# Dequantisation of the feed-forward weights: from the softmax attention's loop into the expert stage

## What is computed

```
x = x + tanh(g_xattn[0]) * linear_attention(layernorm(x), ctx)
x = x + tanh(g_ffn[0])   * experts(layernorm(x))              # 8 experts, top 2, plus a shared one
x = x + tanh(g_xattn[1]) * softmax_attention(layernorm(x), ctx)  # 16 heads, fake-quantised queries and output
x = x + tanh(g_ffn[1])   * feed_forward(layernorm(x), Wg, Wu, Wd)

def dequant_nvfp4(W_packed, scales, block=32):     # Wg, Wu, Wd come packed
    low  = W_packed & 15                           # two 4-bit codes per word
    high = W_packed >> 4 & 15
    idx  = stack([low, high])
    vals = LUT[idx]      # 0 .5 1 1.5 2 3 4 6, and the same negated for codes 8 to 15
    return vals * scales # one scale per 32 values
```

## Time and profile before

| | us |
|---|---|
| median of 3 runs (2783.67 to 2786.23) | 2785.93 |
| the profiled execution | 2784.78 |
| its span, first to last instruction | 2783.1 |
| PE busy | 2628.8 (94%) |
| DVE busy | 1835.6 (66%) |
| POOL busy | 1521.4 (55%) |
| ACT busy | 1487.8 (53%) |

### The profile page before, as it was taken

One profiled execution on the slowest core, in us unless ns is written; L12 is line 12 of the kernel. 1 busy time (PEld: TensorE's weight loads), 2 busy tenths in 40 slices (PEclk: granted clock), 3 DMA queues, 4 the chain that ended last, 5 costly groups with the idle time before them and its releaser, 6 DMA issues. The chain is left out here.

```text
span 2783.1 us, 63103 instructions
## 1 busy us (share of the span) xinstructions
PE 2628.8 (94%) x23470; PEld 2228.8 (80%) x23470; DVE 1835.6 (66%) x3075; ACT 1487.8 (53%) x2543; POOL 1521.4 (55%) x1547
## 2 busy tenths in 40 slices
PE   5999999999899997699999999999999999979998
PEld 3999999999765664488888888888888888858998
DVE  4888888888742225466667666666666666655654
ACT  2666666666321221366666666666666666643443
POOL 2988888888532111456656656656655655632322
PEclk9999999999989998799999999999999999989999
DMA  4554454454381112121121121111112112131000
GB/s 121 165 155 146 141 155 145 142 155 144 79 238 49 46 46 65 51 66 64 34 64 63 34 64 63 35 63 64 45 52 64 58 38 64 41 122 66 8 8 14
DMA packets 110936, 225.25 MB, mean 81 GB/s; under 512 B 32800, under 2 KB 81040, under 8 KB 106864
## 3 DMA queue, kind: packets, MB, share of 16 engines
q1 hardware_dynamic: 105536, 215.86, 25.8%
q0 software_dynamic: 3216, 8.29, 0.9%
q10 hardware_dynamic: 2112, 0.12, 0.1%
HBM read 193.24 MB, written 27.33 MB: 79 GB/s over the span
## 5 line engine op out<-in xcount | busy, mean ns | idle before, releaser
L1607 DVE TENSOR_SCALAR_CACHE_REDUCE a_prob<-a_s 112x1500 f32<-112x1500 f32 x256 | 440.1, 1719 | 116.4 <-PE a_s L1716 115.9
L1728 PEld LDWEIGHTS a_p<-ident,a_prob 112*125 112x125 f32 x3072 | 380.4, 188 | 112.1 <-issue 103.4
L1549 ACT COPY a_probT<-a_p 125x448 f32<-125x448 f32 x512 | 248.8, 534 | 375.3 <-PE a_p L1728 375.3
L1728 PE MATMUL a_p<-ident,a_prob 112*125 112x112 f32 x3072 | 445.6, 281 | 2.2 <-ACT a_prob L1542 1.4
L1542 ACT ACTIVATE a_prob<-a_prob,a_mxs 112x1500 f32<-112x1500 f32 x256 | 396.6, 1549 | 64.8 <-DVE a_prob L1607 64.8
L443 POOL TENSOR_TENSOR l_rows_lo<-l_raw,l_rows_hi 125x512 fp32r<-125x512 f32 x192 | 273.1, 1422 | 104.9 <-ACT l_rows_hi L478 104.9
L446 POOL TENSOR_TENSOR l_phik_lo<-l_phif,l_phik_hi 125x512 fp32r<-125x512 f32 x192 | 297.5, 1550 | 11.8 <-ACT l_phik_hi L484 11.8
L542 DVE TENSOR_TENSOR l_ctxT_lo<-l_rawT,l_ctxT_hi 128x500 fp32r<-128x500 f32 x192 | 214.5, 1118 | 94.9 <-ACT l_ctxT_hi L461 94.8
L80 PE MATMUL l_k<-T_Wk_lo,l_ctxT_hi 128*125 128x256 f32 x768 | 224.2, 292 | 36.9 <-DVE l_phif L559 26.8
L80 PE MATMUL a_a<-T_wv_lo,a_ctxT_hi 128*125 128x256 f32 x768 | 232.0, 302 | 0.0
L1450 POOL TENSOR_TENSOR a_ctxT_lo<-a_rawT,a_ctxT_hi 128x1000 fp32r<-128x1000 f32 x96 | 224.0, 2333 | 7.7
(11 more groups left out here) (313 smaller groups left out, 6947.6 us busy)
## 6 DMA issues: line engine op xcount, KB each, us to landing
l_rawT<-in_ctxT SPq DMA_DIRECT2D x32, 1500.0 KB, 6.3
a_rawT<-in_ctxT SPq DMA_DIRECT2D x32, 1500.0 KB, 6.8
l_raw<-in_ctx SPq DMA_DIRECT2D x32, 1344.0 KB
e_wall<-in_L_ffn_w_gate_up SPq DMA_DIRECT2D x8, 1024.0 KB, 14.1
W_hi<-w_out_hi SPq DMA_DIRECT2D x32, 192.0 KB, 6.6
W_lo<-w_out_lo SPq DMA_DIRECT2D x32, 192.0 KB, 6.5
l_raw<-in_ctx SPq DMA_DIRECT2D x32, 156.0 KB
e_xb<-sorted_x SPq DMA_DIRECT2D x35, 129.0 KB, 2.0
```

The lines of the kernel that those rows point to most:

```text
L1549: act.copy(p_target(j, f), p_source(i)).then_inc(p_read[i], 1)
L1607: dve.tensor_scalar(prob[j % 2][:, :].rearrange("p (g n) -> p g n", g=KG), s_bank[0:TT, :, 0:GW], 1.0, None, ALU.mult, ALU.min, accum_out= ...
L1728: mm = pe.transpose(p_bank[i][0:CH, q * TT:(q + 1) * TT], prob[j % 2][:, ch * CH:(ch + 1) * CH], K["ident"][0:TT, 0:TT])
```

## The change

The dequantisation leaves `softmax_attention` altogether: the entries `A`, `N`, `B`, `U`, `W` of the lists, the code loads and weight stores of SyncE, and the buffers. It enters `experts`, a slice in each of the steps 14 to 45 (`SLICES`). Its buffers lie in `e_xn`, widened from 112 to 128 partitions, whose rows have been scattered by then; so in the new kernel's rows every buffer of it is called `e_xn`, and there is one copy of each.

The computation is laid out anew. VectorE takes magnitude bits and sign bit of both codes apart (four instructions). ACT makes the factor 0.5 - bit/8 (that is 0.5 or -0.5), a float copy of the magnitude, and the two bends (four instructions). VectorE multiplies the factor by the scale. GpSimd adds the two bends, multiplies, rounds to `hi`, subtracts to `lo` (five instructions; before there were nine). The loads and stores are now issued by ACT. GpSimd's scatters of `sorted_y` stand in one sequence with the slices, three steps behind their block's step.

```diff
@@ experts
+        xn_all = c.sb("e_xn", [P, NT, XW])
+        xn = xn_all[0:TT, :, :]
+        w_codes, w_scale = w_at(0, 1).bitcast(I32), w_at(1, 1)
...
+        SLICES = range(W_FIRST, W_FIRST + B)
@@ experts, GpSimd
-            for b in range(NB):
+            def dequantise(s):
+                pool.wait_ge(w_bent, 4 * s + 3)
+                pool.tensor_tensor(w_mag[:, :, :], w_mag[:, :, :], w_four[:, :, :], ALU.add).then_inc(w_sum, 1)
+                pool.wait_ge(w_sum, 3 * s + 1)
+                pool.wait_ge(w_bent, 4 * s + 4)
+                pool.tensor_tensor(w_mag[:, :, :], w_mag[:, :, :], w_six[:, :, :], ALU.add).then_inc(w_sum, 1)
+                pool.wait_ge(w_sum, 3 * s + 2)
+                pool.wait_ge(w_scaled, s + 1)
+                pool.tensor_tensor(w_mag[:, :, :], w_mag[:, :, :], w_factor[:, :, :], ALU.mult).then_inc(w_sum, 1)
+                pool.wait_ge(w_sum, 3 * s + 3)
+                if s:
+                    pool.wait_ge(w_kept, 32 * s)
+                pool.tensor_copy(w_out.hi[:, :, :], w_mag[:, :, :]).then_inc(w_made, 1)
+                pool.wait_ge(w_made, 2 * s + 1)
+                pool.tensor_tensor(w_out.lo[:, :, :], w_mag[:, :, :], w_out.hi[:, :, :].bitcast(F32), ALU.subtract).then_inc(w_made, 1)
+
+            for i in range(FIRST, N + 2):
+                if i in SLICES:
+                    dequantise(slice_of(i))
+                b = i - FIRST - 3
+                if not 0 <= b < NB:
+                    continue
@@ experts, ACT
+            def load_codes(s):
+                if s:
+                    act.wait_ge(w_bits, 4 * s)
+                act.dma_start(w_codes[:, :], a["codes"][:, slice_at(s)]).then_inc(w_in, 16)
+                if s:
+                    act.wait_ge(w_scaled, s)
+                act.dma_start(w_scale[:, :], a["code_scales"][:, slice_at(s)]).then_inc(w_scaled_in, 16)
+            def bend(s):
+                act.wait_ge(w_bits, 4 * (s + 1))
+                if s:
+                    act.wait_ge(w_made, 2 * s)
+                act.activation(w_factor[:, :, :], w_sign[:, :, :], ACT.Identity, scale=-0.125, bias=w_bias[0.5][:, :]).then_inc(w_bent, 1)
+                act.copy(w_mag[:, :, :], w_size[:, :, :]).then_inc(w_bent, 1)
+                act.activation(w_four[:, :, :], w_size[:, :, :], ACT.Relu, bias=w_bias[-4.0][:, :]).then_inc(w_bent, 1)
+                act.activation(w_six[:, :, :], w_size[:, :, :], ACT.Relu, scale=2.0, bias=w_bias[-12.0][:, :]).then_inc(w_bent, 1)
+            def keep_weights(s):
+                act.wait_ge(w_made, 2 * (s + 1))
+                act.dma_start(K["W_hi"][:, :, slice_at(s)], w_out.hi[:, :, :].bitcast(F32)).then_inc(w_kept, 16)
+                act.dma_start(K["W_lo"][:, :, slice_at(s)], w_out.lo[:, :, :].bitcast(F32)).then_inc(w_kept, 16)
             for i in range(N + 1):
                 if i < N:
                     silu(i)
+                if i == FIRST:
...
+                    load_codes(0)
+                if i - 1 in SLICES:
+                    keep_weights(slice_of(i - 1))
+                if i in SLICES:
+                    bend(slice_of(i))
+                if i + 1 in SLICES and i >= W_FIRST:
+                    load_codes(slice_of(i + 1))
                 if i >= 1:
                     turned(i - 1)
@@ experts, VectorE
+            def codes(s):
+                dve.wait_ge(w_in, 16 * (s + 1))
+                if s:
+                    dve.wait_ge(w_bent, 4 * s)
...
+            def factor(s):
+                dve.wait_ge(w_scaled_in, 16 * (s + 1))
+                dve.wait_ge(w_bent, 4 * s + 1)
+                dve.tensor_tensor(w_factor[:, :, :], w_factor[:, :, :], w_scale[:, :].unsqueeze(1).to_broadcast([P, 2, WJ]),
+                                  ALU.mult).then_inc(w_scaled, 1)
@@ experts, VectorE, the loop
                     product(i)
+                if i in SLICES:
+                    factor(slice_of(i))
+                if i + 1 in SLICES:
+                    codes(slice_of(i + 1))
                 if i >= 2:
                     result(i - 2)
@@ the lists
-    "K11 A P00 P01 E1 "
-    "P10 P11 E2 N "
+    "K11 P00 P01 E1 "
+    "P10 P11 E2 "
...
-    "M0 R1' B P72' K10 "
+    "M0 R1' P72' K10 "
...
-    "L1' Q1 U W "
+    "L1' Q1 "
```

More of the change, by code:

```diff
@@ L698, in experts @@
         stepi, below, ones = c.sb("e_stepi", [TT, TT], I32), c.sb("e_below", [TT, TT]), c.sb("e_ones", [TT, TT])
+        w_at = lambda n, m: xn_all[:, :, :].rearrange("p t d -> p (t d)")[:, n * WJ:(n + m) * WJ]
+        w_pair = lambda n: w_at(n, 2).rearrange("p (h n) -> p h n", h=2)
+        w_codes, w_scale = w_at(0, 1).bitcast(I32), w_at(1, 1)
+        w_size, w_sign = w_pair(2).bitcast(I32), w_pair(4).bitcast(I32)
+        w_mag, w_four, w_six, w_factor = w_pair(6), w_pair(8), w_pair(10), w_pair(12)
+        w_out = Parts(w_pair(14).bitcast(F32R), w_pair(16).bitcast(F32R))
+        w_bias = {v: c.sb(f"w_bias{n}", [P, 1]) for n, v in enumerate((-4.0, -12.0, 0.5))}
+        w_in, w_scaled_in, w_bits, w_bent, w_scaled, w_sum, w_made, w_kept, bias_set = (
+            c.sem(f"w_{m}") for m in ("in", "scale_in", "bits", "bent", "scaled", "sum", "made", "kept", "bias_set"))
         g_bank = [c.ps(f"e_g{i}", [P, 512]) for i in range(2)]
@@ L1320, in softmax_attention @@
         second, summed = c.sb("a_second", [P, L]), c.sb("a_summed", [P, L])
[L1321 to L1325, removed]
         s_bank = c.ps("a_s", [P, 3, 512])
@@ L1336, in softmax_attention @@
         linv_done, lsel_done = each("linv_done", KC), each("lsel_done", KC)
-        w_in, w_bits, w_signed, w_part, w_halved, w_bent, w_step, w_valued, w_made, w_kept = (
-            c.sem(f"w_{m}") for m in ("in", "bits", "signed", "part", "halved", "bent", "step", "valued", "made", "kept"))
-        ones_set, masks_set, bias_set = c.sem("a_ones_set"), c.sem("a_masks_set"), c.sem("a_bias_set")
+        ones_set, masks_set = c.sem("a_ones_set"), c.sem("a_masks_set")
         o_at, l_at = slice(0, TT), slice(256, 256 + L)
@@ L1389, in turn_queries, with batch @@
                     sp.dma_start(q_now[0:low, g - 1, :, :], mine[P - low:P, :, :]).then_inc(q_in, 16)
[L1391 to L1402, removed]
+            def batch(b):
                 for g in range(KG):
@@ L1415, in _ @@
             load(0)
-            load_codes(0)
-            batch(0, first=True)
-            with sp.Fori(1, B - 1) as b:
+            with sp.Fori(0, B - 1) as b:
                 batch(b)
[L1420 to L1423, removed]
         @block.gpsimd
@@ L1549, in p_copy @@
                 act.copy(p_target(j, f), p_source(i)).then_inc(p_read[i], 1)
[L1551 to L1561, removed]
-                act.activation(w_six[:, :, :], w_half[:, :, :], ACT.Relu, scale=2.0, bias=w_bias[-6.0][:, :]).then_inc(w_bent, 1)
             def batch(b):
@@ L1654, in batch @@
                         value_copy(of, w)
-                    elif w == "B":
-                        codes(of)
             dve.wait_ge(masks_set, 2)
```

58 lines of the change are left out of this document (13 added, 45 removed).

## The result

The changed kernel takes 2873.19 us (median of four runs, 2870.39 to 2877.78) against 2785.47 for the kernel before in the same comparison: a ratio of 1.0314, 95% interval 1.0302 to 1.0327, or 87.7 us more. Forecast were 2857 us and 71.9 us more. The direction held, and the time lies in the range. The size is 16 us off, and it will turn out that two errors of opposite sign stand in it.

The account below looks back on a forecast made before the run. TensorE was taken to bound both stages: removal 0, a serial ACT-GpSimd chain of 8.20 us a step against 5.82, 32 x 2.38 = 76.2, less 4.3, 71.9 us more than 2784.78, so 2857 us; range 2818 to 2884.

Parts of the forecast that it names:

- the removal: Taking the dequantisation out of the softmax attention's loop, where TensorE's stream covered it: gain taken as 0.
- The loader's 16.67 us of room: TensorE's weight loader, busy 83.33 of 100 us: at most 6.9 us a softmax batch could be gained.
- Rival 1: Softmax batches shorten through freed GpSimd and ACT; half of 6.9 us a batch would give 2747 us; 5%.
- The chain, 8.20 us: Expert steps: stores and activations on ACT, then GpSimd, serial between slices with one buffer set; 8.20 us against 5.82.
- the 4.3 taken off: Deducted from the chain's 76.2 us: about 3 us of slack at the start, 1.3 for stores absent before the first slice.
- The failed step: Claim that neither the codes' loop (5.6 us) nor the blocks' reload loop (7.75 us a step) exceeds the chain's 8.20.
- The reload loop: Expert stage: late scatter releases a block's buffer, then reload, projection, silu, stores; 15.5 us over two steps, 7.75 each.
- I would be wrong if the clock in those steps were under 1.00: Sign against the forecast: TensorE's granted clock falling below 1.00 in the expert steps that carry slices.
- Rival 5: TensorE's clock falls as it idles 2.4 us in each 8.2 us expert step; at worst 186 us more, 2971; 5%.
- Rivals 2 and 4: 2: DMA issues cost ACT little, 2822 us, 10%. 4: factor and GpSimd's additions exclude each other, 2884 us, 8%.
- Rival 3: The added work fits the expert steps by busy sums if slices overlap, so nothing grows: 2786 us; 3%.
- the codes' loop: Expert stage: load_codes issued behind bend, landing, then VectorE's codes before the next bend; 5.6 us, or 8.7 with slower landing.

Follow-up runs that it names:

- x3: Changed kernel without the slices' arithmetic (zeros stored as weights), all four DMAs a slice kept on ACT: 2787.62 us against 2787.02 for the kernel before, ratio 1.0003.
- x4: x1 with a second set of the buffers mag, four, six and factor, and the stores issued behind bend: 2796.44 us, ratio 1.0034 to the kernel before.
- x10: x1 with one more GpSimd instruction a slice between the two additions, waited for like the others: 2868.21 us, ratio 1.0289 to the kernel before.
- x1: Changed kernel with eight buffers xb for the blocks in place of six: 2849.11 us, ratio 1.0223 to the kernel before.
- x5: Changed kernel with four more matmuls a step on TensorE, ahead of the wait for the next block: 2860.50 us, ratio 1.0267 to the kernel before.
- x11: x1 with only the two weight stores of a slice issued by SyncE instead of ACT: 2811.86 us, ratio 1.0086 to the kernel before.
- x6: x4 with GpSimd's first addition given to VectorE and result ahead of codes there: 2786.64 us against 2786.17 for the kernel before, ratio 1.0001.
- x7: x1 with result(i-2) moved ahead of codes(i+1) on VectorE: 2845.68 us, ratio 1.0213 to the kernel before.
- x2: x1 with all four DMAs of a slice issued by SyncE instead of ACT, ahead of a block's reload: 2816.21 us, ratio 1.0105 to the kernel before.

## Why the prediction was right, and where it was not

- **What bounds the kernel; the removal.** Right: TensorE in both stages, 0 for the removal (x3: 0.6 us, within the interval). The loader's 16.67 us of room in 100 were no room. Rival 1 is out.
- **The chain, 8.20 us.** Right in kind (x4, x10), 0.30 too long: 7.90 on average and 7.81 in the turn shown. The stores (1.30) and the activations (1.61) came as priced from the earlier trace rows. GpSimd's part was 5.13 in the sum and is 4.90: the dependent starts in the earlier trace rows lie 1.19 apart, here 1.08 to 1.12. The hand-overs of 0.25 are hardly there: the first store starts at 1013.05 and GpSimd ends at 1013.02, and from ACT to GpSimd the 1.61 hold it. Alone the chain made x1's 62.1 us (2849.11 - 2787.02), 9.8 under the forecast 71.9; by the prediction's own sum, 32 x 2.08 - 4.3 = 62.3, so the 4.3 taken off stood.
- **The failed step: "neither is longer than 8.20, but both are near".** The reload loop was listed with its parts, and two of them were too small. Scatter to turn was 4.4 (2.4 + 2.0) and is 963.40 - 958.24 = 5.16. Both landings are longer in the trace after, with medians of 2.8 us for the scatter and 2.4 for the block; in this step they are 2.79 (to the issue at 961.03) and 2.37. Turn to `silu` was 1.94 and is 4.04, of which x5 shows 1.15 to be the clock (2.89 there). The other 0.95 is for the most part the turn, which the reading of the earlier trace rows left out: 908.41 is the start of VectorE's `result`. In the kernel before, the turn starts at 908.21 and the projection 0.22 us behind it:

```profile
908.21 0.38 PE L1048 MATMUL e_d<-ident,e_xb 128*128 128x128 f32 x2
...
908.43 1.88 PE L1060 MATMUL e_g<-e_wall,e_xT 128*128 x4
```

After a wait for the block the projection starts 0.88 us behind the turn even at full clock (1001.02 and 1001.90 in x5), and 0.85 in the step shown. Why TensorE idles for 0.44 us between the two there stays open; in the program the load of the block's weight offset (`weights_of`) stands between them, and no run takes it out. In return `silu`'s 0.6 runs beside the issue of `W_hi`. At full clock the loop is 16.2 us and not 15.5, worth 11.4 us over the chain by the medians and 6.5 by the steps.
- **The clock.** "I would be wrong if the clock in those steps were under 1.00": it was 0.89 and 0.91, which makes 12.7 us by the medians and 16.6 by the steps. Rival 5 came in part. It was given 5% as a thing of its own; its price needed the failed step first, since the slow projection costs only where it stands in the loop that sets the step. x10 shows the other case: there the clock is 0.90 and 0.91 in the same two windows, TensorE's waits for `y` of over a microsecond are 2.3 to 3.3 us long (900 to 1000), and the time is still the chain's, 19.1 over x1 where the added instruction makes 18.9. In x1, with the same 79.35 busy in 900 to 1000, the clock is 0.98 (0.95 in 1000 to 1100); its waits there are 1.1 to 2.7 us long, those for a block in the changed kernel 2.8 to 5.0.
- **The sum.** 71.9 - 9.8 + 11.4 + 12.7 = 86.2, measured 86 to 88. It closes because its last three terms are differences between the runs, so it is no check of the causes. Two errors in opposite directions kept the forecast close, which was luck: the chain's made it 9.8 us too high, the reload loop's 24 too low.
- **Rivals 2 and 4.** Issues in the chain cost nearly what was said (x11: 37.2 us less without the stores, where 41.6 were counted), and nothing outside it (x3). `factor` has a median of 558 ns, near the lower end worked out from the earlier trace rows, and costs the sum nothing, as taken: GpSimd's first addition has a median of 992 ns beside it, though single ones take up to 1382. Rival 3, that the slices fit if they overlap, was true of the machine but not of this kernel: x6 is that case, at 2786.64.
- **What was to be seen.** TensorE 80% busy and not 70%, and the lower clock is not the whole reason, since x1 has the same 79.35 at 0.98; its waits stood on `e_xb` and not on `e_hT` or `e_y`. With the block in time, in x1, they stood on `e_y`, as forecast.

## What to carry to other kernels

Added busy time said "fits" and was right about the work and wrong about the kernel: with one set of buffers, a loop through two engines costs the sum of its parts and not the larger, and a second set of them, with the stores moved behind `bend` and two more buffers for the blocks, gave back all but 9 of 88 us. Look first at what need not stand in the loop: 37 of these came from moving the two stores to another engine, without a second set. Where two loops come out within 10% of each other, list the parts of the longer-distance one with the same care, with its DMA landings under the new traffic; and where it makes TensorE wait microseconds at a stretch, price its restart at the lower clock in the same loop. A step's waits name who came last there, not what sets the pace: x7 moved 44 us of waits and its median is 3.4 us lower, within the intervals.

## What the runs showed of the hardware

- VectorE's integer `tensor_scalar` with one input in SBUF takes 0.25 us, but 1.05 when it starts while a GpSimd instruction runs (962.18 above): it ends 0.1 us behind that instruction. Under GpSimd's 0.51 us instruction it takes 0.57 (x10). `e_y`, whose tensor input is in PSUM, keeps 468 to 484 ns in all 35 blocks of the changed kernel. The Trainium skill (SBUF — State Buffer, Who interferes with whom) says that `tensor_scalar` can enter modes that take the port pair shared with GpSimd, and that the later one is blocked for the whole of the earlier. The trace agrees, 1.05 against 0.25. The prediction had looked for this lock on `factor` alone; on the four integer operations it did not lengthen the chain (GpSimd's starts are 1.08 to 1.12 us apart in x1, against 1.19 in the earlier trace rows), but where the codes' loop sets the step (x2) it stands in the way.
- A DMA issue on ACT whose wait is already met is issued beside the activations that stand ahead of it in the program (codes at 959.53, `bend` from 959.42 to 961.46), while one that has to wait holds back what stands behind it (`W_hi` 958.12, `bend` 959.42). "Strictly in program order", as said of the engines at the start, is thus too strong for the issues on ACT.
- A GpSimd instruction on 128x384 elements takes 1.0 us with two tensor inputs and 0.51 with one.
